# First layer of a four-layer attention program: where the instance norm's sums are taken, and by which engines

## The chip, the core and the metric

The program runs on 1 core of a Trainium2 chip. The metric is the device time of one execution in microseconds (us); lower is better. Before the change it is 4261.2 us, the median of 3 runs (4258.87 to 4265.15).

## What is computed

Four layers run one after the other on 8 batches; the change touches the first. With `x` and the context of 256 channels by 512 positions per batch, this layer projects queries, keys and values (16 heads of 16), takes a softmax attention over 512 positions, and uses its output's mean and spread to restyle the instance norm of `x`. The part that is changed is that norm:

```python
def _masked_instance_norm(x, mask):
    m = mask.astype(x.dtype)
    x = x * m
    n_valid = jnp.sum(m, axis=-1, keepdims=True)
    mean = jnp.sum(x, axis=-1, keepdims=True) / n_valid
    var = jnp.sum(x * x, axis=-1, keepdims=True) / n_valid - mean * mean
    x = (x - mean) / jnp.sqrt(jax.nn.relu(var) + EPS)
    return x * m
```

The output of the layer, per channel and position, is this norm times the root of the attention's variance (the attention of squared values less the squared attention, clipped at zero), plus the attention itself, times the mask.

## The kernel before

The layer is the function `layer0`. Five engines each run a hand-written list of instructions, tied together by semaphores. Heads are taken in 4 groups of 4 per batch, and every engine has a function `group(b, g)` with a loop over 8 steps `n`; in a step TensorE makes the scores of one pair of heads and one quarter of positions (`scores`, L481), the products whose maxima belong to the group after the next (`maxima`, L461), and weighted values of two steps before (`weighted`, L495). ScalarE takes the exponential of each step's scores (L653), VectorE the maxima (`take_max`, L764). TensorE may not start the next `maxima` before VectorE has read the last one, and not the scores of step n before the exponential of step n-2 is done. Everything else is hung into these steps at fixed places `n`: projections of the next batch in groups 0 and 2 (n = 3 and 4), values in group 3 (n = 5 and 7), transposes of a finished pair (`turn_pair`, L503) at n = 2 and 6. Groups 2, 3, 0, 1 of consecutive batches are the body of a hardware loop, so one period of the loop goes from group 2 of one batch to group 2 of the next.

The norm runs on the transposed rows `XT` (positions on partitions, 4 quarters of 128 positions by 256 channels), so that its result fits the attention's output:
- VectorE's `mask_x` (L801 to L807) copies the mask column and multiplies `XT` by it, half at the end of group 1, half in group 2, n = 0, and sets `stats_read`, after which SyncE may load the next `XT` (`load_statistics`).
- ScalarE squares the result into `XQ` in group 2, n = 5 (L673).
- TensorE's `statistics` (L439), at the end of group 2, multiplies both by a matrix of ones, so that every partition receives the sums over positions, for 256 channels each:

```python
for c in range(EC):
    pe.matmul(ps[:, BX, 0:L], ONES[:, :], XM[:, c, :], start=(c == 0), stop=(c == EC - 1), skip_group_check=True)
```

- VectorE's `moments` and `spread_of_x` (L809 to L822), in group 3, n = 0, scale the sums by the reciprocal of the valid count and form the variance, 256 columns wide. `count_valid` (L734) counts the mask on VectorE.
- GpSimd's `centre` (L323) subtracts the mean in group 3.
- ScalarE's `roots` (L681 to L685), in group 0 of the next batch behind n = 5 and the copy of that group's first pair, takes the root of the variance (256 columns) and of the attention's variance `VAR` (1024 columns). Each switch between exponential and root is a table load.
- VectorE's `inverse_root` (L874) takes reciprocals in two halves, GpSimd multiplies by `VAR` (L335), by the reciprocals (`scale`, L329), adds the attention (`shift`, L339), masks (L345) and stores.

For the last batch VectorE's `last_output` (L878) does all of the last part, and SyncE stores (L274). Layer 2 of the program starts behind that store.

SyncE issues nearly all transfers in one fixed order: in the loop, strips of group 1, maxima, `load_statistics`, `load_inputs`, queries and keys to scratch memory, strips of group 2, maxima, strips of group 3, and so on (L247 to L261). An entry that waits holds up all behind it.

## Time and profile before

| | |
|---|---|
| runs (3) | 4258.87, 4261.2, 4265.15 us |
| profiled execution | 4272.13 us, span 4270.5 us |
| mean granted clock of TensorE | 0.974 of full speed |
| TensorE busy in the span | 4003.9 us (94%) |
| VectorE, ScalarE, GpSimd busy | 2937.2, 1937.1, 1590.8 us |
| last store of the first layer issued at | 693.8 us |

The profile is of one execution. A row of a timeline gives start and duration in us, then engine, line, operation and tiles, and in brackets how long the engine sat idle before it and what ended that. Durations overlap a little: the next instruction of an engine often starts some 0.1 us before the last one's end. `PE` is TensorE, `DVE` VectorE, `ACT` ScalarE, `POOL` GpSimd, `SPq` SyncE's queue.

### The profile page before, as it was taken

The page shows a single profiled execution, that of the slowest core. Times are in us where ns is not written, and L with a number is a line of the kernel's source. Part 1 is how long each engine was busy: PE and PEld are TensorE (multiplying, and loading weights), DVE is VectorE, ACT ScalarE, POOL GpSimd, SP SyncE. Part 2 cuts the span into 40 slices and gives each one's busy share as a digit, 9 for nine tenths or more (in the row PEclk, how much of TensorE's full clock was granted, in tenths as well). Part 3 has the DMA queues.
Part 4 walks back from the last instruction along what each step waited for, and adds up shares of the span by engine and source line. Part 5 has one row for each costly group of instructions (what it writes and reads, how often), then busy time and mean ns, then how long its engine had stood idle before and what let it go on. Part 6 is the DMA issues. An engine that isn't in the chain of part 4 may idle for free. (4 is left out here: it accounts for less than half of the span.)

```text
span 4270.5 us, 68365 instructions
## 1 busy us (share of the span) xinstructions
PE 4003.9 (94%) x20812; PEld 3017.2 (71%) x20812; DVE 2937.2 (69%) x6467; ACT 1937.1 (45%) x3782; POOL 1590.8 (37%) x1094
## 2 busy tenths in 40 slices
PE   6999996789999987999999999999999999999999
PEld 2343333567777755887977888977988877878866
DVE  5667663688888893775757766757757757757643
ACT  2566563223333322555552555543555534555522
POOL 1334331456666651232235232344332244232230
PEclk7999998899999998999999999999999999999999
DMA  5434433000000002212123222223221122121122
GB/s 149 131 111 119 128 90 129 6 11 16 16 16 16 11 11 74 70 60 80 60 65 104 70 65 76 65 63 107 65 82 64 55 76 93 60 90 61 56 79 99
DMA packets 159994, 298.65 MB, mean 70 GB/s; under 512 B 19781, under 2 KB 42821, under 8 KB 158545
## 3 DMA queue, kind: packets, MB, share of 16 engines
q1 hardware_dynamic: 158000, 290.86, 21.9%
q0 software_dynamic: 1008, 3.67, 0.2%
q8 instruction: 119, 1.95, 0.2%
q10 hardware_dynamic: 752, 1.23, 0.1%
q14 instruction: 115, 0.93, 0.1%
HBM read 254.28 MB, written 42.21 MB: 69 GB/s over the span
## 5 line engine op out<-in xcount | busy, mean ns | idle before, releaser
L2177 POOL TENSOR_TENSOR c_wl<-c_wr,c_wh 128x512 fp32r<-128x512 f32 (+1 forms) x576 | 821.5, 1438 | 1641.9 <-ACT c_wh L2544 1385.2
L2645 ACT ACTIVATE c_pr<-c_ps,c_nms 128x257 f32<-128x257 f32 x512 | 244.5, 477 | 482.0 <-DVE c_nms L2867 480.1
L1701 DVE TENSOR_TENSOR_SCAN b_sb<-b_wt,b_s,b_ps 128x256 f32<-128x256 f32 x512 | 361.6, 736 | 16.3 <-PE b_ps L1154 4.4
L764 DVE TENSOR_REDUCE a_nm<-a_ps 128x2 f32<-128x1024 f32 x256 | 311.5, 1221 | 63.1 <-PE a_ps L461 61.2
L653 ACT ACTIVATE a_ex<-a_ps 128x1024 f32<-128x1024 f32 x256 | 260.3, 1023 | 181.4 <-PE a_ps L481 180.3
L1652 POOL TENSOR_TENSOR b_sb<-b_sb,b_rt 128x1024 f32<-128x1024 f32 x128 | 278.0, 2179 | 156.5 <-DVE b_sb L1701 122.4
L2544 ACT ACTIVATE c_wh<-c_wr 128x512 fp32r<-128x512 f32 (+1 forms) x464 | 315.3, 687 | 44.4 <-PE c_ps L2264 40.7
L2262 PE MATMUL c_ps<-c_hh,c_wh 128*128 128x512 f32 x768 | 309.6, 403 | 12.4 <-DVE c_hl L2751 12.0
L2262 PE MATMUL c_ps<-c_gh,c_wh 128*128 128x512 f32 x768 | 307.6, 400 | 5.4 <-DVE c_gl L2909 2.7
L2264 PE MATMUL c_ps<-c_hh,c_wl 128*128 128x512 f32 x768 | 304.5, 397 | 0.0
L2263 PE MATMUL c_ps<-c_hl,c_wh 128*128 128x512 f32 x768 | 304.2, 396 | 0.0
L2262 PE MATMUL c_ps<-c_wh,c_cth 128*128 128x256 f32 x1024 | 303.5, 296 | 0.0
L2264 PE MATMUL c_ps<-c_gh,c_wl 128*128 128x512 f32 x768 | 303.3, 395 | 0.0
L2263 PE MATMUL c_ps<-c_gl,c_wh 128*128 128x512 f32 x768 | 302.9, 394 | 0.0
L2264 PE MATMUL c_ps<-c_wh,c_ctl 128*128 128x256 f32 x1024 | 288.3, 282 | 0.0
L2263 PE MATMUL c_ps<-c_wl,c_cth 128*128 128x256 f32 x1024 | 287.7, 281 | 0.0
L495 PE MATMUL a_ps<-a_ex,a_vf 128*64 128x512 f32 x1024 | 278.6, 623 | 1.4 <-ACT a_ot L645 1.3
L2865 DVE TENSOR_REDUCE c_nm<-c_ps 128x1 f32<-128x257 f32 x512 | 215.1, 420 | 71.8 <-PE c_ps L2264 71.4
L1166 PE MATMUL b_ps<-b_xf,b_w 128*128 128x256 f32 x1056 | 244.1, 385 | 12.1 <-DVEq L1760 10.1
L1166 PEld LDWEIGHTS b_ps<-b_xf,b_w 128*128 128x128 f32 x1056 | 200.3, 192 | 46.3 <-issue 14.4
L2909 DVE TENSOR_TENSOR c_gl<-c_g,c_gh 128x512 fp32r<-128x512 f32 x128 | 90.7, 713 | 206.3 <-ACT c_gh L2627 206.1
L2861 DVE TENSOR_SCALAR c_pr<-c_pr,c_rs 128x257 f32<-128x257 f32 x512 | 195.0, 381 | 42.0 <-issue 3.1
(371 smaller groups left out, 10087.0 us busy)
## 6 DMA issues: line engine op xcount, KB each, us to landing
c_wr<-in_downs SPq DMA_DIRECT2D x192, 256.0 KB, 2.7
c_wr<-in_wv SPq DMA_DIRECT2D x64, 512.0 KB, 4.0
c_wr<-in_wk SPq DMA_DIRECT2D x128, 256.0 KB, 2.9
c_wr<-in_wq SPq DMA_DIRECT2D x128, 256.0 KB, 2.6
a_qp<-strips SPq DMA_DIRECT2D x64, 256.0 KB, 4.1
a_kp<-strips SPq DMA_DIRECT2D x64, 256.0 KB, 4.9
c_wr<-in_fc SPq DMA_DIRECT2D x64, 256.0 KB, 2.8
strips<-a_qh SPq DMA_DIRECT2D x32, 256.0 KB
```

The source lines that it names most:

```text
L495: mm = pe.matmul(ps[64 * a:64 * a + VCOLS, BO, :], VF[:, k, g * HG + 2 * p + a, :], EX[:, n % 4, a, :], start=(k == 0), stop=(k == EC - 1) ...
L653: act.activation(EX[:, n % 4, :, :], ps[:, BT + 2 * (n % 2):BT + 2 * (n % 2) + 2, :], ACT.Exp).then_inc(ex_ready, 1)
L764: dve.tensor_reduce(NM[:, s, :].rearrange("p (h c) -> p h c", h=HG)[:, 2 * p:2 * p + 2, c:c + 1], ps[:, bank:bank + 2, :], AX.X, ALU.max, ...
L1166: mm = pe.matmul(half(bank, o), W[:, w, k, o * P:(o + 1) * P], src[:, k, :], start=(k == 0), stop=(k == EC - 1), skip_group_check=True)
L1652: pool.tensor_tensor(SB[:, quad % RING, :, :, 0:L], SB[:, quad % RING, :, :, 0:L], RT[:, third(b, q // 8)].unsqueeze(1).broadcast_to([P, 2 ...
L1701: mm = dve.tensor_tensor_scan(SB[:, quad % RING, pr % 2, e, 1:L + 1], WT[:, third(b, i), e, :], half(spread_bank(pair), e), S0[:, b % 2, 2 ...
L2177: pool.tensor_tensor(piece(WL, slot), piece(WR, slot), piece(WH, slot), ALU.subtract).then_inc(piece_cut[slot], 1)
L2262: pe.matmul(out, sh, mh, start=start, stop=False, skip_group_check=True)
L2263: pe.matmul(out, sh, ml, start=False, stop=False, skip_group_check=True)
L2264: return pe.matmul(out, sl, mh, start=False, stop=stop, skip_group_check=True)
L2544: act.activation(piece(WH, slot), piece(WR, slot), ACT.Copy).then_inc(piece_high[slot], 1)
L2645: act.activation(PR[:, i, 0:L + 1], ps[:, BS + 1 - i % 2, 0:L + 1], ACT.Exp, bias=NMS[:, i:i + 1], scale=float(K2) ** -0.5, accum_out=RS[: ...
```

## The change

The sums are no longer taken from the transposed rows by TensorE, but from the rows `X` as they are loaded for the projections (channels on partitions, 2 halves of 128 by 512 positions), so that each sum is one column.
- VectorE's `sum_inputs` multiplies a half by the mask row and adds it up (one half at the end of group 1, one in group 2, n = 0, for the batch after). ScalarE's `square_inputs` squares the product with a sum (group 2, n = 1 and 2), `count_valid` moves to ScalarE (group 1, n = 4).
- ScalarE's `column_moments` (group 3, n = 3) scales the four sums and forms the clipped variance on columns; `roots` now takes the root of 2 columns of the same batch besides that of `VAR` of the batch before, VectorE's `inverse_root` the reciprocal of 2 columns (group 1, n = 6).
- TensorE's `statistics` transposes mean and reciprocal root, each column repeated 128 times, back into rows: four transposes. VectorE's `take_rows` copies them out.
- GpSimd's `normalize` subtracts and multiplies in group 3, from the unmasked `XT`; `centre` and `scale` go. `stats_read` is now set by its first product.
- SyncE's `load_statistics` stands behind group 0's maxima instead of ahead of `load_inputs`; `load_inputs` waits for `x_summed` and `counted`.
- The conversions `cut_x` and `cut_c` on ScalarE are made in halves, `square_values` moves from n = 2 to n = 6, in group 0 ahead of `cut_c`; GpSimd's `cut_c` stands ahead of `copy_values(b, 1)`.
- For the last batch GpSimd does the first three groups' part of the output, VectorE the last group's, after waiting for GpSimd.

The diff, cut to its core:

```diff
@@ load_inputs, SyncE
-                sp.wait_ge(mask_read, b + AHEAD)
+                sp.wait_ge(x_summed, b * LC + AHEAD)
+                sp.sem_inc(passed, 1)
+                sp.wait_ge(counted, b + AHEAD)
@@ SyncE's loop
                 place_maxima(b, 3)
-                load_statistics(b + 1)
                 load_inputs(b + 2)
...
                 place_maxima(b + 1, 0)
+                load_statistics(b + 1)
                 place_strips(b + 1, 3)
@@ GpSimd
+            def normalize(b):
+                pool.wait_ge(st_read, b + 1 + AHEAD)
+                pool.wait_ge(stats_x_in, (b + 1) * N_STATS + AHEAD)
+                pool.tensor_tensor(XM[:, :, :], XT[:, :, :], ST[:, 0:1, :].broadcast_to([P, EC, L]), ALU.subtract)
+                pool.drain().then_inc(stats_read, 1)
+                pool.tensor_tensor(XM[:, :, :], XM[:, :, :], ST[:, 1:2, :].broadcast_to([P, EC, L]), ALU.mult)
...
+            cols = slice(0, (G0 - 1) * CG)
+            pool.wait_ge(std_ready, B + AHEAD)
+            pool.tensor_tensor(XM[:, :, cols], XM[:, :, cols], VAR[:, :, cols], ALU.mult)
+            pool.tensor_tensor(XM[:, :, cols], XM[:, :, cols], MEAN[:, :, cols], ALU.add)
+            for c in range(EC):
+                pool.tensor_scalar(OUT[:, c, cols], XM[:, c, cols], MCOL[:, c:c + 1], None, ALU.mult)
+            pool.drain().then_inc(parts_out, 1)
@@ statistics, TensorE
-                for c in range(EC):
-                    pe.matmul(ps[:, BX, 0:L], ONES[:, :], XM[:, c, :], start=(c == 0), stop=(c == EC - 1), skip_group_check=True)
-                for c in range(EC):
-                    mm = pe.matmul(ps[:, BX, L:2 * L], ONES[:, :], XQ[:, c, :], start=(c == 0), stop=(c == EC - 1), skip_group_check=True)
+                for i, k in itertools.product(range(2), range(LC)):
+                    mm = pe.transpose(ps[:, BX, i * L + k * P:i * L + (k + 1) * P], COLS[:, i, k:k + 1].broadcast_to([P, P]), ID[:, :])
@@ ScalarE
+            def count_valid(b):
+                act.activation(JUNK[:, :], M8R[:, :], ACT.Copy, accum_out=NV[:, :]).then_inc(counted, 1)
+            def column_moments(b):
+                act.wait_ge(rn_ready, b + 1 + AHEAD)
+                act.wait_ge(x_squared, (b + 1) * LC + AHEAD)
+                act.wait_ge(st_ps, b + AHEAD)
+                act.activation(COLS[:, :, :], SUMS[:, :, :], ACT.Copy, scale=RN[:, 0:1])
+                act.drain()
+                act.activation(MSQ_X[:, :], COLS[:, 0, :], ACT.Square)
+                act.drain()
+                for k in range(LC):
+                    act.activation(COLS[:, 1, k:k + 1], MSQ_X[:, k:k + 1], ACT.Relu, scale=-1.0, bias=COLS[:, 1, k:k + 1])
+                act.drain()
+            def square_inputs(b, k):
+                act.wait_ge(x_summed, b * LC + k + 1 + AHEAD)
+                act.activation(XS[:, k, :], XS[:, k, :], ACT.Square, accum_out=SUMS[:, 1, k:k + 1]).then_inc(x_squared, 1)
-                act.activation(ST[:, 3, :], ST[:, 2, :], ACT.Sqrt, bias=EPS[:, 0:1])
+                act.activation(COLS[:, 1, :], COLS[:, 1, :], ACT.Sqrt, bias=EPS[:, 0:1]).then_inc(root_x, 1)
@@ VectorE
+            def sum_inputs(b, k):
+                if k == 0:
+                    dve.wait_ge(inputs_in, (b + 1) * N_IN + AHEAD)
+                dve.tensor_tensor_reduce(XS[:, k, :], X[:, k, :], M8R[:, :], 1.0, 0.0, ALU.mult, ALU.add, SUMS[:, 0, k:k + 1]).then_inc(x_summed, 1)
+            def inverse_root(b):
+                dve.reciprocal(COLS[:, 1, :], COLS[:, 1, :]).then_inc(cols_ready, 1)
+            def take_rows(b):
+                dve.wait_ge(st_ps, b + 1 + AHEAD)
+                dve.tensor_copy(ST[:, :, :], ps[:, BX, :].rearrange("p (s t) -> p s t", s=2)).then_inc(st_read, 1)
```

How the order moves, on TensorE at the end of group 2: `L481` are scores, `L461` products for maxima, `L495` weighted values, `L446` and `L448` the products with ones. Before:

```order
L503 MATMUL a_ps<-a_id,a_ot 128x128 x4
L477 REGISTER_ALU
L481 MATMUL a_ps<-a_qp,a_kp 128x512 x2
L458 REGISTER_ALU
L461 MATMUL a_ps<-a_kp,a_qp 128x512 x2
L495 MATMUL a_ps<-a_ex,a_vf 64x512 x2
L441 REGISTER_ALU
L446 MATMUL a_ps<-a_xm,a_ones 128x256 x4
L448 MATMUL a_ps<-a_xq,a_ones 128x256 x4
L475 ISA
L477 ISA
L481 MATMUL a_ps<-a_qp,a_kp 128x512 x2
```

And now (`L460` are the transposes of the columns):

```order
L515 MATMUL a_ps<-a_id,a_ot 128x128 x4
L489 REGISTER_ALU
L493 MATMUL a_ps<-a_qp,a_kp 128x512 x2
L470 REGISTER_ALU
L473 MATMUL a_ps<-a_kp,a_qp 128x512 x2
L507 MATMUL a_ps<-a_ex,a_vf 64x512 x2
L456 REGISTER_ALU
L460 MATMUL a_ps<-a_id,a_cols 128x128 x4
L487 ISA
L489 ISA
L493 MATMUL a_ps<-a_qp,a_kp 128x512 x2
```

Eight products of 256 columns gave way to four of 128; nothing else moved on TensorE. On VectorE, at the border of groups 1 and 2 (the loop begins at the branch; `a_nm` are the maxima), before:

```order
L764 TENSOR_REDUCE a_nm<-a_ps 128x2
L801 CAST a_mcol<-a_m8c 128x4
L804 TENSOR_SCALAR a_xm<-a_xT,a_mcol 128x256 x2
L925 UNCONDITIONAL_BRANCH
L925 ISA
L764 TENSOR_REDUCE a_nm<-a_ps 128x2
L804 TENSOR_SCALAR a_xm<-a_xT,a_mcol 128x256 x2
L763 REGISTER_ALU
L764 TENSOR_REDUCE a_nm<-a_ps 128x2
```

And now:

```order
L829 TENSOR_REDUCE a_nm<-a_ps 128x2
L783 ISA a_xs,a_sums<-a_x,a_m8r 128x512
L783 ISA a_sums 128x1
L945 UNCONDITIONAL_BRANCH
L945 ISA
L829 TENSOR_REDUCE a_nm<-a_ps 128x2
L783 ISA a_xs,a_sums<-a_x,a_m8r 128x512
L783 ISA a_sums 128x1
L828 REGISTER_ALU
L829 TENSOR_REDUCE a_nm<-a_ps 128x2
```

Each pair of masked quarters became one multiply-and-sum in two instructions, and the mask column's copy left this place.

## Rows read from the trace of the kernel before

**Rows 1.** Windows, one period: PE, PEld, DVE, ACT, POOL busy, clock, DMA share, GB/s

```profile
340.08:418.81 78.73, 75.20 (x357) 30.83 (x357) 54.66 (x75) 47.29 (x56) 30.23 (x31) 1.00 0.41 122
```

**Rows 2.** TensorE's groups by line, 200 to 650 us: busy, mean ns, idle before

```profile
L461 PE MATMUL a_ps<-a_kp,a_qp 64*128 64x512 f32 x368 | 81.8, 441 | 12.6 <-DVE a_nm L764 12.6
```

**Rows 3.** Timeline of TensorE, 340 to 402 us: the rows with a wait

```profile
340.08 0.51 PE L461 MATMUL a_ps<-a_kp,a_qp 64*128 64x512 f32 x2 [0.65 <-DVE a_nm L764]
...
363.33 0.49 PE L461 MATMUL a_ps<-a_kp,a_qp 64*128 64x512 f32 x2 [0.32 <-DVE a_nm L764]
...
365.74 0.49 PE L461 MATMUL a_ps<-a_kp,a_qp 64*128 64x512 f32 x2 [0.27 <-DVE a_nm L764]
...
400.38 0.50 PE L481 MATMUL a_ps<-a_qp,a_kp 64*128 64x512 f32 x2 [1.09 <-ACT a_ex L653]
```

**Rows 4.** Timeline of TensorE, end of group 2

```profile
354.92 0.66 PE L503 MATMUL a_ps<-a_id,a_ot 128*128 128x128 f32 x4
355.51 0.50 PE L481 MATMUL a_ps<-a_qp,a_kp 64*128 64x512 f32 x2
...
357.18 1.99 PE L446 MATMUL a_ps<-a_xm,a_ones 128*128 128x256 f32 x8
...
360.83 0.51 PE L481 MATMUL a_ps<-a_qp,a_kp 64*128 64x512 f32 x2
```

**Rows 5.** Timeline of VectorE, groups 1 to 3

```profile
336.21 1.23 DVE L764 TENSOR_REDUCE a_nm<-a_ps 128x2 f32<-128x1024 f32 x1
...
338.82 1.21 DVE L764 TENSOR_REDUCE a_nm<-a_ps 128x2 f32<-128x1024 f32 x1
...
363.19 0.42 DVE L817 TENSOR_TENSOR a_st<-a_st 128x256 f32<-128x256 f32 x1
```

**Rows 6.** Groups by line and form, VectorE and ScalarE, whole span

```profile
L793 DVE TENSOR_TENSOR a_vs<-a_ps,a_bvb 128x512 f32<-128x512 f32 x16 | 11.1, 692 | 25.1 <-PE a_ps L436 25.1
...
L1817 DVE SCALAR_TENSOR_TENSOR b_zb<-b_zb,b_xb 128x1024 f32<-128x1024 f32 x6 | 7.3, 1218 | 0.0
...
L2645 ACT ACTIVATION_READ_ACCUMULATOR c_pr<-c_ps,c_nms 128x1 f32 x512 | 98.7, 193 | 0.0
```

**Rows 7.** Timeline of ScalarE, then one row of TensorE, groups 3 and 0

```profile
369.97 1.02 ACT L653 ACTIVATE a_ex<-a_ps 128x1024 f32<-128x1024 f32 x1 [0.56 <-PE a_ps L481]
...
383.92 0.60 ACT L645 ACTIVATE a_ot<-a_ps 128x512 f32<-128x512 f32 x1
...
395.24 1.28 ACT L683 ACT_TABLE_LOAD   x1
396.54 0.51 ACT L683 ACTIVATE a_st<-a_st,a_eps 128x256 f32<-128x256 f32 x1
...
399.30 1.02 ACT L653 ACTIVATE a_ex<-a_ps 128x1024 f32<-128x1024 f32 x1
...
374.69 0.50 PE L481 MATMUL a_ps<-a_qp,a_kp 64*128 64x512 f32 x2
```

**Rows 8.** Tail of the layer: ScalarE, SyncE; GpSimd's masking by line

```profile
685.54 0.83 ACT L715 ACTIVATE a_var<-a_var 128x768 f32<-128x768 f32 x1
...
693.82 0.35 SPq L274 DMA_DIRECT2D x1T<-a_xq  x1
...
L345 POOL TENSOR_SCALAR a_xq<-a_xm,a_mcol 128x256 f32<-128x256 f32 x28 | 25.4, 918 | 1.2 <-issue 1.2
```

**Rows 9.** GpSimd and SyncE in group 3; first batch's head; the page's issues

```profile
371.58 2.38 POOL L323 TENSOR_TENSOR a_xm<-a_xm,a_st 128x1024 f32<-128x1024 f32 x1
...
377.54 1.31 SPq L224 DMA_DIRECT2D a_qp<-strips  x2
...
12.46 2.35 POOL L294 TENSOR_TENSOR a_cl<-a_ctx,a_ch 128x1024 fp32r<-128x1024 f32 x1 [9.56 <-ACT a_ch L631]
...
12.78 2.18 DVE L729 TENSOR_SCALAR a_mbrr<-a_m8r 128x256 fp32r<-128x256 uint8 x1 [0.20 <-issue]
...
a_kp<-strips SPq DMA_DIRECT2D x64, 256.0 KB, 4.9
```

More of the change, by code:

```diff
@@ L97, in layer0 @@
         ID = sb("id", [P, P])
-        ONES = sb("ones", [P, P])
         EPS = sb("eps", [P, 1])
@@ L116, in layer0 @@
         MSQ = sb("msq", [P, EC, HG, D0])
-        ST = sb("st", [P, 4, L])
+        ST = sb("st", [P, 2, L])
         NV = sb("nv", [P, 1])
         RN = sb("rn", [P, 1])
+        SUMS = sb("sums", [P, 2, LC])
+        COLS = sb("cols", [P, 2, LC])
+        MSQ_X = sb("msq_x", [P, LC])
+        XS = sb("xs", [P, 2, E])
+        JUNK = sb("junk", [P, E])
         OUT = XQ
@@ L653, in group @@
                     act.activation(EX[:, n % 4, :, :], ps[:, BT + 2 * (n % 2):BT + 2 * (n % 2) + 2, :], ACT.Exp).then_inc(ex_ready, 1)
+                    if g == 0 and n == 0 and not first:
+                        square_values(b, 0)
+                    if g == 0 and more and n == 0:
+                        cut_c(b + 1, 0)
+                        cut_c(b + 1, 1)
                     if n == 1 and not first:
@@ L658, in group @@
                             take_pair(b - 1, G0 - 1, 1)
[L659 to L661 removed]
+                    if n == 6 and g + 1 < G0:
                         square_values(b, g + 1)
+                    if g == 2 and more and n in (1, 2):
+                        square_inputs(b + 1, n - 1)
+                    if g == 1 and more and n == 4:
+                        count_valid(b + 1)
                     if more and g % 2 == 0 and n == QUERIES_AT:
@@ L668, in group @@
                         keys(b + 1, g // 2)
-                    if g == 2 and n == 5:
-                        act.wait_ge(stats_in, b + 1 + AHEAD)
-                        act.wait_ge(out_free, b + AHEAD)
-                        act.activation(XQ[:, :, :], XM[:, :, :], ACT.Square).then_inc(sq_ready, 1)
-                    if g == 0 and n == 0 and not first:
-                        square_values(b, 0)
-                    if g == 0 and n == 5 and prior is not None:
-                        roots(prior)
@@ L678, in group @@
-                    if g == G0 - 1 and n == 5 and further:
-                        cut_x(b + 2)
-            def roots(b):
-                act.wait_ge(var_x, b + 1 + AHEAD)
-                act.activation(ST[:, 3, :], ST[:, 2, :], ACT.Sqrt, bias=EPS[:, 0:1])
-                act.wait_ge(var_v, (b + 1) * G0 + AHEAD)
-                act.activation(VAR[:, :, :], VAR[:, :, :], ACT.Sqrt).then_inc(std_ready, 1)
+                    if g == G0 - 1 and more and n == 3:
+                        column_moments(b + 1)
@@ new lines, in group @@
+                    if g == 0 and n == 5:
+                        roots(b, prior)
+                    if g == G0 - 1 and n in (5, 6) and further:
+                        cut_x(b + 2, n - 5)
+            def count_valid(b):
+                act.wait_ge(inputs_in, (b + 1) * N_IN + AHEAD)
+                act.activation(JUNK[:, :], M8R[:, :], ACT.Copy, accum_out=NV[:, :]).then_inc(counted, 1)
[10 more added lines that the diff above has]
+                act.drain()
@@ L687, in _ @@
             act.wait_ge(wqk_in, 16 + AHEAD)
             act.activation(WH[:, :, :, 1, :], WQK[:, :, :, 1, :], ACT.Copy).then_inc(wk_high, 1)
-            cut_x(0)
-            cut_c(0)
+            for k in range(LC):
+                cut_x(0, k)
+            for k in range(LC):
+                cut_c(0, k)
             act.wait_ge(weights_split, 2 + AHEAD)
@@ L695, in _ @@
             keys(0, 1, BT + 3)
+            count_valid(0)
             square_values(0, 0)
-            cut_x(1)
+            for k in range(LC):
+                square_inputs(0, k)
+            column_moments(0)
+            for k in range(LC):
+                cut_x(1, k)
             group(0, 0, first=True)
@@ L826, in group @@
                     if g == G0 - 1 and n == 0:
-                        moments(b)
+                        take_rows(b)
                     if left > 1:
@@ L850, in group @@
                         mask_rows(1, 1)
-                    if first and n == 5:
-                        count_valid(1)
                     if g == G0 - 1 and further and n == 1:
@@ L915, in _ @@
             dve.tensor_tensor(WVL[:, :, :], WV, WVH[:, :, :], ALU.subtract).then_inc(wv_split, 1)
+            for k in range(LC):
+                sum_inputs(0, k)
+            count_inverse(0)
             take_values(0, 0, BO)
```

158 lines of the change are left out of this document (62 added, 96 removed).

## The prediction

> **What bounds the kernel.** The change touches only the first layer, the first 694 of 4270.5 us, so I read the windows of that layer first. One batch repeats every 78.73 us, and TensorE is busy for 75.20 of them, at a granted clock of 1.00, that is 2.4 GHz; VectorE has 54.66, ScalarE 47.29, GpSimd 30.23 [rows 1]. TensorE is the bound, and its order is written out by hand, so what is taken from it or from its waits shortens the loop one for one, as long as nobody else becomes late. Second, TensorE's groups by line between 200 and 650 us (5.7 batches) tell what it waits for ahead of the products whose maxima VectorE takes: 12.6 us for VectorE, nothing for a transfer [rows 2]. Third, its timeline shows where in a batch these waits lie. Four bear on the change: 0.65 us at 340.08, 0.32 at 363.33, 0.27 at 365.74, and, for ScalarE's exponential, 1.09 at 400.38 [rows 3]. The first is also the start of the next period (it comes back at 418.81).
>
> **The change, part by part.** All times are of the batch between 340 and 419 us; the other six like it are the same to some hundredths.
>
> *Column sums on TensorE.* The eight products with the matrix of ones start at 357.18 (the first four in 8 passes), and the next scores start at 360.83: 3.65 us. In their place stand four transposes of 128 columns. The four of a pair of heads, same shape and type, start at 354.92 and let the next product start at 355.51: 0.59 us [rows 4]. That the stationary side is one column repeated has no row; bounds are 0.59 and, if each went in two passes as the ones' products do, 1.2. I take 0.59, the same form. 3.06 us less, in all 8 batches (the last too: nothing else runs on TensorE there), is 24.5 us; with 1.2 it is 19.6.
>
> *VectorE at the border of groups 1 and 2.* The last maximum of group 1 ends at 337.44 (336.21 + 1.23), then mask column and two masked quarters run, the first maximum of group 2 starts only at 338.82, and TensorE waits 0.65 us for its end [rows 5, 3]. Now one multiply-and-sum of 128x512 stands there, and another after that maximum. No row shows the form. Lower bound: one pass, a two-input operation of 128x512, 0.69; upper: two passes, 1.38. The order shows a second instruction that fetches the sum; VectorE has no row of one, ScalarE's takes 0.19 [rows 6]. I take one pass, 0.69 + 0.16 less 0.1 of overlap, 0.75: two-input operations are the nearest rows, and all of them run in one pass. Then the first maximum starts at 338.2, ends at 339.4, and TensorE, which comes at 339.43, hardly waits: 0.6 won. The second sum ends at 340.2 and the maximum behind it at 341.4, about when TensorE asks again (a step later; two such steps lie 2.4 us apart between 363.33 and 365.74, and this one is a little shorter): free. In 7 batches (the last takes no maxima there): 4.2 us. Upper bound of the price: 1.4 each gives back all of the 0.6 and adds 0.6 at the next maximum, so 4.2 less and 4.2 more lost, 8.4 between the ends.
>
> *VectorE at the start of group 3.* Two scaled copies, two products, a clip, and a reciprocal become one copy of 128x512, about 0.68 by its width [rows 6]. Both waits come from them: the first maximum came behind the scaled copies, the second behind the variance from 363.19 [rows 5]. With 0.7 the first wait shrinks to about 0.1, the second goes: 0.49 in 7 batches, 3.4 us. If the copy takes 1.0, 0.3 a batch comes back (2 us).
>
> *ScalarE at the roots.* Table load 1.28, root of the moments' 256 columns (0.51 busy, 0.41 to the next start), root of the values, load, and the exponential at 399.30 holds TensorE 1.09 us [rows 7, 3]. The first root now has 2 columns, about 0.2 (ScalarE's smallest form takes 0.19 [rows 6]), 0.1 of it overlapped: 0.3 less, 7 times, 2.1 us. The added roots in the very first group cost 2.8 us of ScalarE; the later ones (4.1 us) overrun TensorE by 1.09, so 3.0 is free, and this costs nothing. If that cover were gone, 2.8 once.
>
> *ScalarE elsewhere.* The halved conversion of the context costs one extra start, 0.12, right ahead of the pair copy of 383.92 [rows 7], for which TensorE is just in time: 0.1 x 7, 0.7 us lost. Count of the mask, two squares with sum (0.63 + 0.19 each) and the column work (four of 0.2, and three drains, no row, 0 to 0.3 each: 0.8 to 1.7) fall into steps with one exponential of 1.02 us, in an engine that is idle for 31 of 78.7 us; the exponential behind the column work starts at 369.97 and ends 1.02 later, and the scores that need it come at 374.69 [rows 7], so up to 3.7 us are hidden. The square of the masked rows (1.05) goes. Nothing on the path.
>
> *GpSimd and queues.* Centring and scaling stay two products of 2.38; both are now in group 3, so the output is stored some 5 us earlier. The load of rows and mask column moved behind a maximum's placement, and waits for GpSimd's first product: a rival below. The inputs' load comes one transfer sooner. All hidden under TensorE.
>
> *Head and tail.* Head: conversions in halves, 0.1; the sums lie in VectorE's 3 us of idle time before the first values. Tail: before, the store is issued at 693.82. Now ScalarE's root of 768 columns ends 0.41 earlier, at 685.96; GpSimd then does two products of 768 columns (3/4 of 2.38, 1.78 each) and four of 192 (0.69 to 0.92 each), so 6.3 to 7.2 us, to 692.3 to 693.2; VectorE, waiting for it, adds two operations of 256 columns (0.42 each) and four small ones: store at 693.9 to 695.6 [rows 8, 5]. I take 1.2 us lost: this part gains nothing, GpSimd is the slower engine for it.
>
> Sum: 24.5 + 4.2 + 3.4 + 2.1 - 0.7 - 1.2 = **32.3 us less**. The profiled execution took 4272.1 us, 10.9 above the median shown; against the median, 4261.2 - 32.3 = **4228.9**.
>
> **A rule weighed.** In the first batch VectorE took 2.18 us for 256 columns of mask rows, where a two-input operation of 512 takes 0.69 [rows 6], and it ended (14.96) as GpSimd's product of 12.46 did (14.81) [rows 9]: the two engines do block each other. The new sums read two SBUF tensors. In before GpSimd worked until 339.6 at this place, because its output chain waited for VectorE's reciprocals; without scaling there it is done 3.5 us before the sums, so I charge nothing. If it overlapped, its step of 0.74 us would be added, at most 7 x 0.7 = 5 us. The Trainium skill, page "SBUF — State Buffer", in its practical consequences, says that a VectorE instruction with two SBUF inputs contends with a GpSimd instruction that reads SBUF, the later one waiting in full; by it alone the overlapping case holds and the sum is 27. The trace agrees with blocking (2.18 us); where GpSimd will be is the open point.
>
> **Rivals.**
> *A, the sums are slow on VectorE.* Two passes, 1.4 us each: VectorE delays TensorE in two steps. 32.3 - 8.4 = 23.9, time **4237**. For it: the form has no row and carries an accumulator. Against: the product of two 128x512 tensors and the maxima over 1024 columns run in one pass. The Trainium skill, "Vector Engine (DVE) Microarchitecture Reference", in its list of pitfalls, says that this family with two SBUF sources that are not bf16 runs at half throughput, leaving no port for the accumulator; by that rule this rival is the outcome. A three-operand form of 128x1024 takes 1218 ns here [rows 6], which is full rate, but without an accumulator.
>
> *B, transposes cost double.* 24.5 becomes 19.6: **4234**.
>
> *C, slower: the SyncE queue stands behind GpSimd.* The load of rows and mask column now waits on SyncE for GpSimd's first product, which in before ran from 371.58 to 373.96. Behind it is queued the placement of group 3's strips, issued at 377.54 in before [rows 9]. TensorE asks for these strips at about 400.7; issuing the four takes 2.6 (twice 1.31) and landing 4.9 [rows 9], so the placement may slip to about 393, and the product's end, with 1.2 us for two issues, to about 392: 18 us later than now. Beyond that point each us costs 7. To eat 32.3 us it would have to be 23 us late. GpSimd has 48 us idle in a batch and depends there only on pair 1 of group 2 and on the copied rows, so I see no way; if it does happen, with 28 us of delay, the time is about **4299** (7 x 10 - 32.3 more).
>
> *D, no change:* freed TensorE time returns as waits on transfers. TensorE waited for none in the loop; 4261.
>
> **How the numbers follow.** The sum as it stands, 4224 to 4234: 0.58. A, including port blocking: 0.27. B: 0.06. More than summed (further waits for VectorE go too, tail even): 4221, 0.03. C: 0.02, slower. D: 0.04. The predicted time is 4229. The range, 4221 to 4241, takes in A and B with 2 to 4 us for their own bounds. A measurement of this kernel tells 0.2% (8.5 us) from no change: faster 0.94, same 0.04, slower 0.02.
>
> **What would show it.** Right: the transposes of the columns start 0.6 us ahead of the next scores; period 74.3 to 74.5 us; no wait left at the two places of group 3 and at the border of groups 1 and 2; the wait after the roots near 0.8; the store of the last batch 30 to 33 us earlier than 693.82. Wrong: a multiply-and-sum above 1.2 us and a wait in its place (A); transposes over 1 us together (B); TensorE waiting for strips in group 1 (C), or for any transfer (D).

## The result, and the profile after

The changed kernel took **4228.4 us**, median of 4 runs (4223.6 to 4230.6), beside 4262.1 us for the kernel before in the same comparison (4258.9 to 4265.2): a ratio of 0.9916, with a 95% interval of 0.9904 to 0.9928. That is 31 to 41 us less, 33.7 by the medians. Measured twice more, it gave 4228.3 (ratio 0.9916, 0.990 to 0.9933) and 4231.4 us (0.9927, 0.9914 to 0.9941).

The period of the loop is now 73.80 us instead of 78.73 [rows 1]. The windows view of one (here from the wait behind the keys in group 2 to the same place of the next batch), with the columns of [rows 1]:

```profile
337.27:411.07 73.80, 71.62 (x345) 28.25 (x346) 51.29 (x68) 48.80 (x67) 30.15 (x31) 1.00 0.44 129
```

TensorE is busy for 3.58 us less (75.20 to 71.62), VectorE for 3.37, ScalarE for 1.51 more. The other 1.35 us of the 4.93 are time in which TensorE waited. In its groups by line, 200 to 620 us (about the same 5.7 batches as [rows 2], now shorter), idle time for VectorE fell from 12.6 to 6.0 us:

```profile
L493 PE MATMUL a_ps<-a_qp,a_kp 64*128 64x512 f32 x370 | 92.2, 495 | 6.0 <-ACT a_ex L671 6.0
L473 PE MATMUL a_ps<-a_kp,a_qp 64*128 64x512 f32 x362 | 79.0, 433 | 6.3 <-DVE a_nm L829 6.0
```

TensorE's timeline at the end of group 2 and the start of group 3. The four transposes start at 340.96 and the next scores 0.58 us behind them, where 3.65 passed before [rows 4], and the two waits of 0.32 and 0.27 in group 3 [rows 3] are gone. The wait of 0.60 in the first row is none of these: it stands behind the low halves of the keys, and the kernel before had it too, at 353.49, with the same length.

```profile
337.27 0.49 PE L473 MATMUL a_ps<-a_kp,a_qp 64*128 64x512 f32 x2 [0.60 <-DVE a_nm L829]
...
340.96 0.65 PE L460 MATMUL a_ps<-a_id,a_cols 128*128 128x128 f32 x4
341.54 0.50 PE L493 MATMUL a_ps<-a_qp,a_kp 64*128 64x512 f32 x2
...
343.21 0.50 PE L493 MATMUL a_ps<-a_qp,a_kp 64*128 64x512 f32 x2
343.60 0.50 PE L473 MATMUL a_ps<-a_kp,a_qp 64*128 64x512 f32 x2
...
345.25 0.50 PE L493 MATMUL a_ps<-a_qp,a_kp 64*128 64x512 f32 x2
345.58 0.39 PE L473 MATMUL a_ps<-a_kp,a_qp 64*128 64x512 f32 x2
```

Later in the period two more waits are left, one behind the keys in group 0 and one behind the roots, the latter 0.88 us instead of 1.09. The three are all that the period has in brackets:

```profile
375.33 0.50 PE L473 MATMUL a_ps<-a_kp,a_qp 64*128 64x512 f32 x2 [0.60 <-DVE a_nm L829]
...
379.98 0.50 PE L493 MATMUL a_ps<-a_qp,a_kp 64*128 64x512 f32 x2 [0.88 <-ACT a_ex L671]
```

The 0.65 at the border of groups 1 and 2 is gone, though not to the last tenth. The product for the maxima starts 0.57 us behind its scores there, where an undisturbed step of this kind has 0.38 (349.17 and 349.56, for one), so some 0.2 us of waiting is left that no bracket shows:

```profile
323.40 0.49 PE L493 MATMUL a_ps<-a_qp,a_kp 64*128 64x512 f32 x2
323.97 0.50 PE L473 MATMUL a_ps<-a_kp,a_qp 64*128 64x512 f32 x2
```

VectorE where the first of the two new sums stands (one batch), and the copy that starts group 3:

```profile
322.08 0.69 DVE L783 CUSTOM_DVE_ANT_0 a_xs<-a_x,a_m8r 128x512 f32<-128x512 f32 x1 [0.18 <-issue]
322.69 0.08 DVE L783 DVE_READ_ACCUMULATOR2_ANT a_sums<- 128x1 f32 x1
322.69 1.22 DVE L829 TENSOR_REDUCE a_nm<-a_ps 128x2 f32<-128x1024 f32 x1
...
341.65 0.69 DVE L795 COPY a_st<-a_ps 128x512 f32<-128x512 f32 x1 [0.34 <-PE a_ps L460]
```

The multiply-and-sum is one pass: 0.69 us, and 0.08 for the read of its sum; the copy is 0.69. Over the whole trace the sixteen sums lie between 678 and 692 ns.

ScalarE at the roots. The root of two columns takes 0.29 us, where the 256 columns that it replaced took 0.51 [rows 7]: only 0.22 us went with the other 254.

```profile
375.05 1.28 ACT L724 ACT_TABLE_LOAD   x1
376.34 0.29 ACT L724 ACTIVATE a_cols<-a_cols,a_eps 128x2 f32<-128x2 f32 x1
376.55 1.04 ACT L727 ACTIVATE a_var<-a_var 128x1024 f32<-128x1024 f32 x1
377.61 1.28 ACT L671 ACT_TABLE_LOAD   x1
378.90 1.02 ACT L671 ACTIVATE a_ex<-a_ps 128x1024 f32<-128x1024 f32 x1
```

**Where the 33.7 us lie.** The profiled executions of before and after differ by more than the medians, so two marks are used that are in every trace: the first statistic product (or transpose) of batch 0, and the issue of the layer's last store.

| us | before | after | difference |
|---|---|---|---|
| first statistic pass | 121.0 | 119.5 | -1.5 |
| last store issued | 693.82 | 655.63 | -38.2 |
| between the two | 572.8 | 536.1 | **-36.7** |
| from the store to the end of the span | 3576.7 | 3566.3 | -10.4 |
| span | 4270.5 | 4221.9 | -48.6 |

The two profiled executions differ by 48.6 us, since that of before came out long. The stretch between the marks is the one that repeats: in two more executions of the changed kernel it was 536.1 and 536.2 us. Of before only this one execution was profiled, and it holds 1.4 us that belong to no term. Behind the last roots TensorE waits 1.81 us, until 633.75, and its next instructions are slow; the granted clock between 636.0 and 637.4 is 0.50 of full speed, that is 1.2 GHz:

```profile
634.41 1.93 PE L495 MATMUL a_ps<-a_ex,a_vf 128*64 128x512 f32 x4
```

Elsewhere this row takes 1.08 us. The kernel of experiment 1 has the same wait of 1.81 there and no slow stretch behind it, and no profiled execution of the changed kernel has one in this layer. The start of the layer varied over 2.6 us between the three executions of the changed kernel, and what comes behind the store, where no instruction changed, lay between 3566 and 3577 us over all the kernels below. So the layer gained 36.7 us between the marks, 35.3 without the slow stretch, and the medians 33.7; the interval of the latter (31 to 41) holds both. The experiments are read by the stretch between the marks, with the medians beside it.

### The profile page after: what moved, and what is told of

It is laid out like the page before. It is cut to its first block and busy times, and to the rows that moved or that the text cites. A ratio compares the mean times of both kernels' runs of the same rounds, so it can differ in the third digit from the quotient of the medians.

```text
span 4221.9 us, 68235 instructions
## 1 busy us (share of the span) xinstructions
PE 3965.2 (94%) x20716; PEld 2988.3 (71%) x20716; DVE 2910.6 (69%) x6417; ACT 1949.7 (46%) x3872; POOL 1601.2 (38%) x1100
```

## The experiments

My theory at this point: the gain is the sum of the terms, with TensorE's 3.07 us a batch by far the largest, and VectorE and GpSimd hidden. Rivals: the gain needs the sums' place on VectorE and not the shorter passes; or the layer is now bound by waits so that more or less TensorE work no longer tells.

**1. Only fewer products.** The kernel before, with two of the eight products with ones; it leaves out three quarters of each column sum and keeps all else.

```diff
-                for c in range(EC):
-                    pe.matmul(ps[:, BX, 0:L], ONES[:, :], XM[:, c, :], start=(c == 0), ...)
-                for c in range(EC):
-                    mm = pe.matmul(ps[:, BX, L:2 * L], ONES[:, :], XQ[:, c, :], start=(c == 0), ...)
+                pe.matmul(ps[:, BX, 0:L], ONES[:, :], XM[:, 0, :], start=True, stop=True, ...)
+                mm = pe.matmul(ps[:, BX, L:2 * L], ONES[:, :], XQ[:, 0, :], start=True, stop=True, ...)
```

> The kernel before, with only one of the four quarters in each of the two column sums: two products with ones instead of eight (the sums of three quarters of the positions are left out, nothing else moves). Theory, TensorE's time counts one for one and the other gains are VectorE's and ScalarE's own: the two products take 0.9 us instead of 3.65, the period falls by 2.7 from 78.73 to 76.0, the two long steps at the start of group 3 (2.47 and 2.79 us) and the one at the border of groups 1 and 2 stay, the time falls by 22 us, to about 4240. Rival, the freed time returns in waits on VectorE, whose scaled copies and variance still follow: the steps of group 3 grow, and less than 11 us are won.

Measured: 4246.4 us, ratio 0.9957 (0.9941 to 0.9974). Between the marks 550.9 us, 21.9 less than before. Its TensorE timeline, from the last products of the statistics:

```profile
348.81 0.59 PE L446 MATMUL a_ps<-a_xq,a_ones 128*128 128x256 f32 x2
349.33 0.50 PE L479 MATMUL a_ps<-a_qp,a_kp 64*128 64x512 f32 x2
...
351.83 0.51 PE L459 MATMUL a_ps<-a_kp,a_qp 64*128 64x512 f32 x2 [0.32 <-DVE a_nm L762]
...
354.24 0.51 PE L459 MATMUL a_ps<-a_kp,a_qp 64*128 64x512 f32 x2 [0.26 <-DVE a_nm L762]
...
388.89 0.51 PE L479 MATMUL a_ps<-a_qp,a_kp 64*128 64x512 f32 x2 [1.08 <-ACT a_ex L651]
```

The two products that are left take 1.06 us until the next scores (348.27 to 349.33) instead of 3.65, so 2.59 us are spared, 20.7 in 8 batches. The other 1.2 us are the slow stretch that only the profiled execution of before has (1.4), less small changes of other steps. What TensorE is spared arrives in the time one for one, with the waits of [rows 3] in place at nearly their old lengths (0.63 for the 0.65). So six of the eight products carry 20.7 us, and the waits are a gain of their own.

**2. More transposes.** The changed kernel, with the four transposes issued six times over.

```diff
-                for i, k in itertools.product(range(2), range(LC)):
+                for _, i, k in itertools.product(range(6), range(2), range(LC)):
```

> The changed kernel with the four transposes made six times over: 20 more at 0.147 us, so 2.94 us of TensorE given back per batch, nothing else. Theory: the period rises from 73.81 to 76.75, the time by 23.5 us, to about 4252; the steps at the start of group 3 stay at 2.04 and 2.25 us, so that the rest of the gain (about 10 us against the kernel before) remains. Rival, the gain hangs on VectorE's shorter lists alone: the time stays near 4228.

Measured: 4249.1 us, ratio 0.9964 (0.995 to 0.9978). Between the marks 553.7 us, 17.6 more than the changed kernel, where I had expected 23.5:

```profile
345.45 2.83 PE L460 MATMUL a_ps<-a_id,a_cols 128*128 128x128 f32 x24
348.21 0.50 PE L493 MATMUL a_ps<-a_qp,a_kp 64*128 64x512 f32 x2
```

24 of them take 2.76 us until the next scores, the first four 0.58: each further one costs (2.76 - 0.58) / 20 = 0.11 us. My expectation had 0.147, the 0.59 divided by four, which spreads the group's fixed part over its members. The added 2.18 us are 17.4 in 8 batches, and 17.6 came. TensorE is still the bound in the changed kernel, one for one, and rival B has no ground.

**3. Sums twice.** The changed kernel, each multiply-and-sum preceded by one into a tile of no use.

```diff
+                dve.tensor_tensor_reduce(XD[:, k, :], X[:, k, :], M8R[:, :], 1.0, 0.0, ALU.mult, ALU.add, SD[:, k:k + 1])
                 dve.tensor_tensor_reduce(XS[:, k, :], X[:, k, :], M8R[:, :], 1.0, 0.0, ALU.mult, ALU.add, SUMS[:, 0, k:k + 1]).then_inc(x_summed, 1)
```

> The changed kernel with every multiply-and-sum on VectorE made twice (the first one into tiles that nobody reads): 0.69 us more at each of the two places. Theory, VectorE stands right behind TensorE at the border of groups 1 and 2, and a sum of 1.4 us is what my rival A priced: TensorE waits about 0.6 us at each of the two steps, the period rises by 1.2, the time by 8.4, to about 4237. Rival, VectorE has 24 us idle per period and takes it in: no change, 4228.

Measured: 4240.4 us, ratio 0.9943 (0.9926 to 0.9959). Between the marks 542.7 us, 6.6 more. Two waits appeared at the border:

```profile
402.89 0.50 PE L475 MATMUL a_ps<-a_kp,a_qp 64*128 64x512 f32 x2 [0.68 <-DVE a_nm L832]
...
405.25 0.50 PE L475 MATMUL a_ps<-a_kp,a_qp 64*128 64x512 f32 x2 [0.21 <-DVE a_nm L832]
```

They make 0.89 us. By distance the two steps are 1.09 us longer (0.61 and 0.48), and six of the seven borders lie between the marks, the first batch's ahead of them: 6.4 of the 6.6 us. This is the price that rival A would have had, not 8.4: VectorE works 0.62 us longer at each of the two places, 1.24 together, and behind the second sum there was 0.1 to 0.2 us of slack.

**4. The tail on VectorE.** GpSimd's share of the last batch's output moved to VectorE, the masking in one operation of 256 columns for each part instead of 192 and 64. The last rows of the changed kernel's layer, GpSimd's and VectorE's:

```profile
646.71 1.86 POOL L404 TENSOR_TENSOR a_xm<-a_xm,a_var 128x768 f32<-128x768 f32 x1 [4.14 <-ACT a_var L762]
646.99 1.73 DVE L913 TENSOR_SCALAR a_var<-a_msq 128x256 f32<-128x256 f32 x1
648.71 1.80 POOL L406 TENSOR_TENSOR a_xm<-a_xm,a_mean 128x768 f32<-128x768 f32 x1
648.75 0.42 ACT L764 ACTIVATE a_var<-a_var 128x256 f32<-128x256 f32 x1 [2.22 <-DVE a_var L913]
650.69 2.99 POOL L409 TENSOR_SCALAR a_xq<-a_xm,a_mcol 128x192 f32<-128x192 f32 x4 [0.18 <-issue]
653.76 0.43 DVE L916 TENSOR_TENSOR a_xm<-a_xm,a_var 128x256 f32<-128x256 f32 x1 [5.04 <-POOLq L410]
...
655.63 0.35 SPq L283 DMA_DIRECT2D x1T<-a_xq  x1
```

VectorE waits 5.04 us for an engine that does the same work at half its rate.

```diff
-            pool.tensor_tensor(XM[:, :, cols], XM[:, :, cols], VAR[:, :, cols], ALU.mult)
...
-            pool.tensor_tensor(XM[:, :, cols], XM[:, :, cols], MEAN[:, :, cols], ALU.add)
...
-                pool.tensor_scalar(OUT[:, c, cols], XM[:, c, cols], MCOL[:, c:c + 1], None, ALU.mult)
...
+                dve.tensor_tensor(XM[:, :, first], XM[:, :, first], VAR[:, :, first], ALU.mult)
...
+                dve.tensor_tensor(XM[:, :, first], XM[:, :, first], MEAN[:, :, first], ALU.add)
...
-                    dve.tensor_scalar(OUT[:, c, cols], XM[:, c, cols], MCOL[:, c:c + 1], None, ALU.mult)
+                    dve.tensor_scalar(OUT[:, c, :], XM[:, c, :], MCOL[:, c:c + 1], None, ALU.mult)
```

> The changed kernel with the whole output of the last batch on VectorE again (no reciprocals there, since the scaling is done in group 3), nothing on GpSimd. Theory, the tail lost because GpSimd takes 6.6 us for what VectorE does in 3.4 and they work one after the other: the store is issued at 651.5 to 652.5 instead of 655.6, the time falls by 3.5 us. Rival, the tail waits for ScalarE's roots anyway: no change in the store.

Measured: 4226.4 us, ratio 0.9912 (0.9895 to 0.9928), beside 4228.3 and 0.9916 for the changed kernel on the same chip. The medians can't tell them apart; between the marks it is 531.75 us, 4.35 less, where 3 to 4 were expected. The end of VectorE's timeline:

```profile
644.65 0.29 DVE L904 TENSOR_SCALAR a_var<-a_msq 128x256 f32<-128x256 f32 x1
644.86 0.95 DVE L908 TENSOR_TENSOR a_xm<-a_xm,a_var 128x768 f32<-128x768 f32 x1
...
647.60 1.14 DVE L916 TENSOR_SCALAR a_xq<-a_xm,a_mcol 128x256 f32<-128x256 f32 x4
```

768 columns take 0.95 us here and 1.86 on GpSimd. The first row shown took 1.73 us in the changed kernel (646.99 to 648.72), while GpSimd's product stood beside it (646.71 to 648.57), and 0.29 here with GpSimd idle.

**5. The keys one step later.** The two waits of 0.60 us left for VectorE stand right behind the low halves of the keys; here VectorE makes these a step later.

```diff
-                    if more and g % 2 == 0 and n == KEYS_AT:
+                    if more and g % 2 == 0 and n == KEYS_AT + 1:
```

> The changed kernel with VectorE's low part of the keys taken behind the maximum of step 5 instead of ahead of it. Theory, the waits of 0.60 us of TensorE in groups 0 and 2 (337.27, 375.33) come from a maximum that stands behind the keys, which wait for ScalarE: both go, the period falls by 1.2 to 72.6, the time by 8 to 9 us. Rival, the keys' later low part delays the transposes of step 6, which wait for it: no gain.

Measured: 4221.3 us, ratio 0.9899 (0.9883 to 0.9916). Between the marks 531.9 us, 4.2 less than the changed kernel, half of what was expected. Both waits went, and the one for ScalarE took over half of it:

```profile
372.85 0.50 PE L493 MATMUL a_ps<-a_qp,a_kp 64*128 64x512 f32 x2 [1.55 <-ACT a_ex L671]
```

0.88 became 1.55. By distance, each step whose wait of 0.60 went is 0.68 us shorter. In group 2 this is won, 4.1 us in the six batches whose keys lie between the marks. In group 0 all 0.68 come back one step later, at the roots. ScalarE's chain of copy, load, root, root, load and exponential does not depend on the keys' low halves; TensorE simply arrives at it earlier.

**6. The roots ahead of the keys.** The same wait from the other side: ScalarE takes the roots one step earlier, and the pair's copy behind the keys' high halves.

```diff
-                    if n == 5:
+                    if n == 5 and g > 0:
                         take_pair(b, g, 0)
+                    if g == 0 and n == KEYS_AT:
+                        roots(b, prior)
                     if more and g % 2 == 0 and n == KEYS_AT:
                         keys(b + 1, g // 2)
+                    if g == 0 and n == KEYS_AT:
+                        take_pair(b, g, 0)
...
-                    if g == 0 and n == 5:
-                        roots(b, prior)
```

> The changed kernel with ScalarE's roots moved from behind step 5's pair copy to ahead of the keys' conversion in step 4, where TensorE projects and ScalarE is idle for 1.7 us; the first pair's copy comes right behind the keys. Theory: the wait of 0.88 us in group 1 goes, and at most 0.3 us comes back before the transposes of step 6: the period falls by 0.6 to 0.9, the time by 4 to 6 us. Rival, the keys come 2 us late and TensorE waits for them: no gain or slower.

Measured: 4230.1 us, ratio 0.9914 (0.9898 to 0.9931), no difference from the changed kernel. Between the marks 535.5 us, 0.6 less, where 4 to 6 were expected. ScalarE's wait is gone, and VectorE's in the same group grew from 0.60:

```profile
375.45 0.50 PE L473 MATMUL a_ps<-a_kp,a_qp 64*128 64x512 f32 x2 [1.36 <-DVE a_nm L831]
```

VectorE's low halves need ScalarE's high halves, which now come behind the roots; its maxima stand behind them. By distance, 0.94 us a batch are won at the roots, 0.76 lost at the maxima and 0.17 in the step behind. Experiments 5 and 6 together say that group 0's wait behind the keys and the wait behind the roots are one knot: whichever is taken alone, the other grows. The wait behind the keys of group 2 is no part of it.

**7. The rows queued early.** Rival C in one move: on SyncE, the load of rows and mask column goes ahead of the placement of group 2's strips and of group 0's maxima. It can't go as far ahead as in the kernel before, where it stands ahead of the inputs. By the code, its release needs GpSimd's product, and this comes behind moments that VectorE takes only behind the next mask rows (`mask_rows`), which wait for the inputs and for keys written by entries behind it on this queue. That was read from the code, not run.

```diff
+                load_statistics(b + 1)
                 place_strips(b + 1, 2)
                 place_maxima(b + 1, 0)
-                load_statistics(b + 1)
                 place_strips(b + 1, 3)
```

> The changed kernel with the load of the transposed rows two entries earlier on SyncE, ahead of the strips of group 2 and the maxima that follow, still waiting for GpSimd's first product. This is the mechanism of my rival C with its slack taken away. Theory: strips and maxima go out only after the product's end (353.7 in the changed kernel) and land at about 362, where TensorE asks at 360: some 2.3 us of waits on a transfer in each of 7 batches, the time up by 16 us, to about 4244. Rival, nothing is behind it in time: 4228.

Measured: 4265.8 us, ratio 1.0002 (0.9992 to 1.0012). Between the marks 573.6 us, 37.5 more than the changed kernel: this one move gives the whole gain back, where I had expected 16. SyncE's timeline in it, then two rows of TensorE's:

```profile
375.03 0.36 SPq L186 DMA_DIRECT2D a_m8c<-in_mask_col  x1
375.61 0.39 SPq L187 DMA_DIRECT2D a_xT<-in_xT  x1
376.29 1.30 SPq L233 DMA_DIRECT2D a_qp<-strips  x2
377.64 1.24 SPq L233 DMA_DIRECT2D a_kp<-strips  x2
379.08 2.62 SPq L196 DMA_DIRECT2D a_qp<-a_nmT  x4
```

```profile
384.92 0.50 PE L493 MATMUL a_ps<-a_qp,a_kp 64*128 64x512 f32 x2 [3.80 <-DMA a_qp<-a_nmT]
...
385.58 1.97 PE L507 MATMUL a_ps<-a_ex,a_vf 128*64 128x512 f32 x4
```

The load leaves when GpSimd's first product is done (372.37 + 2.38 = 374.75), and strips and maxima follow in one block, the strips 18.0 us behind the wait at the keys of group 2 (358.30); TensorE reaches the scores that need these maxima 3.80 us too soon.

That wait is not the whole cost. The second row is an instruction that takes 1.08 us in the changed kernel. While TensorE stood (380.9 to 384.9) its granted clock was 1.00; between 387.0 and 388.6 it was 0.50, the lower of its two levels, 1.2 GHz, and from 390 on 1.00 again. The edit stands in the loop, which runs 6 times. All six times TensorE waits, for 3.80 to 5.34 us, and the steps behind the wait are 1.3 to 2.7 us longer than in the changed kernel. The waits lengthen their steps by 27.0 us in all, the slow steps add 10.9. My expectation had the waits too short (2.3 us each), one batch too many, and no slow stretch at all.

In the changed kernel the same strips left at 344.20, 6.9 us behind that wait, and the maxima at 346.99, both before that product (351.32 to 353.69). The load followed it by 0.29 us without holding up anybody:

```profile
353.98 0.36 SPq L186 DMA_DIRECT2D a_m8c<-in_mask_col  x1
354.55 0.38 SPq L187 DMA_DIRECT2D a_xT<-in_xT  x1
357.28 1.30 SPq L233 DMA_DIRECT2D a_qp<-strips  x2
```

The queue is free again at 354.93, and the next strips wait for a reason of their own until 357.28: 2.35 us of slack, before a transfer that TensorE needs much later.

**8. All three.** Experiments 4, 5 and 6 in one kernel.

> The changed kernel with the three edits of the last call together: tail on VectorE, keys' low part behind the maximum of step 5, roots ahead of the keys' conversion. Apart, the later keys took away both waits of 0.60 us but raised the wait for ScalarE from 0.88 to 1.55, and the earlier roots took that wait away but raised the one for VectorE from 0.60 to 1.36. Theory, each hides what the other left: no wait of TensorE above 0.3 us in the period, which falls by 2.1 us, the tail by 4.4 us, so the time by 19 us, to about 4209. Rival, the late keys now hold up the transposes of step 6: less than 9 us.

Measured: **4214.6 us** (4212.2 to 4217.9), ratio 0.9884 (0.9869 to 0.990), beside 4231.4 and 0.9927 (0.9914 to 0.9941) for the changed kernel on the same chip. Between the marks 522.8 us: 13.4 less than the changed kernel and 50 less than before. The parts alone sum to 4.35 + 4.2 + 0.6 = 9.2. The knot in group 0 is worth 4.9 us when both of its waits are taken, and 0 and 0.6 when one is; group 2's wait gives 4.1 here as in experiment 5, the tail 4.5. The one wait of the period that is left:

```profile
372.51 0.50 PE L484 MATMUL a_ps<-a_qp,a_kp 64*128 64x512 f32 x2 [0.67 <-ACT a_ex L662]
```

I had expected 19 us, with all waits gone. 0.67 in six batches is 4.0 of the missing 5.6, and one pair of the waits behind the keys that I had counted seven times, 1.2, lies outside the marks.

**9. GpSimd beside the sums.** The changed kernel, with three products of 128x1024 on GpSimd behind its copy of the values in group 2, which nobody reads.

```diff
+                for _ in range(3):
+                    pool.tensor_tensor(PD[:, :, :], PS[:, :, :], PS[:, :, :], ALU.mult)
+                    pool.drain()
```

> The changed kernel with three idle products of 128x1024 on GpSimd (7.2 us, into a tile that nobody reads) behind the copy of group 3's values, so that GpSimd reads SBUF while VectorE makes its two sums (322.1 to 324.5 in the changed kernel); GpSimd is otherwise idle from 318.7 to 328.9. Theory, the two-input sums wait for the GpSimd product that has started: a sum is recorded with up to 2.4 us more, TensorE waits in group 2, and the time rises by 7 to 20 us, to 4235 to 4248. Rival, they do not meet: 4228 and sums of 0.69 us.

Measured: 4237.2 us, ratio 0.9942 (0.9927 to 0.9957). Between the marks 542.3 us, 6.2 more, a little under the 7 to 20 expected. VectorE, then GpSimd:

```profile
324.78 1.15 DVE L789 CUSTOM_DVE_ANT_0 a_xs<-a_x,a_m8r 128x512 f32<-128x512 f32 x1 [0.17 <-issue]
...
327.00 1.23 DVE L789 CUSTOM_DVE_ANT_0 a_xs<-a_x,a_m8r 128x512 f32<-128x512 f32 x1
```

```profile
323.49 4.19 POOL L379 TENSOR_TENSOR a_pd<-a_pdum 128x1024 f32<-128x1024 f32 x2 [0.24 <-issue]
```

Two GpSimd products lie in that row. The second ends at 327.68, and the second sum, begun at 327.00, ends at 328.23, 0.55 later. The first product, taken by itself, is 1.89 us long; it ended at 325.38, and the first sum at 325.93, again 0.55 later. A sum alone takes 0.69, so it did nearly all of its work after its neighbour was done. The maxima between, 1.21 us, read no SBUF and are not lengthened beside the same products. The ten sums between 200 and 600 us averaged 1259 ns instead of 685. The two steps of TensorE at the border grew by 0.4 to 0.8 and by 0.3 to 0.4 us at each of the six borders between the marks, together 6.1 us, and no other step did: the 6.2 us are the price of the blocked sums.

## Why the prediction was right

The forecast was 4229 us, and 4228.4 came; its sum was 32.3 us, the layer gave 36.7, or 35.3 without the slow stretch of before, and the medians 33.7. Part of the closeness is luck: the terms fell short by 3 us, and the medians by less. Two of the prediction's own signs missed on the good side, the period (73.80 us, not 74.3 to 74.5) and the last store (38.2 us earlier, not 30 to 33). Point by point, in its own steps; the measured column adds up the steps of TensorE between the marks, from one score to the next, batch by batch:

| term, us | forecast | measured | by |
|---|---|---|---|
| column sums on TensorE | 24.5 | 24.6 | 3.65 to 0.58, 8 times |
| border of groups 1 and 2 | 4.2 | 4.2 | 0.57 + 0.18 in most of the 6 between the marks |
| start of group 3 | 3.4 | 6.5 | 0.97, 7 times, less in the last |
| roots | 2.1 | 1.5 | 1.09 to 0.88, 7 times |
| context in halves | -0.7 | -0.4 | -0.07, 6 times |
| all other steps | none | 0.2 | each below 0.1 a batch |
| slow stretch of before | none | 1.4 | once, in this execution |
| tail | -1.2 | -1.25 | last moments to store, 8.49 to 9.74 |
| sum | 32.3 | 36.7 | 36.7 between the marks |

*Column sums: right in size and mechanism.* The transposes of a repeated column start 0.58 us ahead of the next scores, as those of a pair do (0.59 [rows 4]). Experiment 1 shows that such time comes out of the loop one for one, experiment 2 that it still does in the changed kernel.

*Border: right, with two errors that cancel.* The wait is nearly gone, as forecast. The step with the wait shrank by 0.57 us, and the one behind it, which I had put as free, by 0.18. I counted seven batches; the first one's border lies ahead of the first mark and had only a wait of 0.26. The multiply-and-sum, taken as 0.75, is 0.69 + 0.08.

*Start of group 3: the term that was mis-sized most.* I took TensorE's recorded waits, 0.32 + 0.27, less 0.1 for a rest of the first. No rest stayed, and the two steps shrank by 0.97 (2.47 to 2.04 and 2.79 to 2.25), more than the waits recorded in them. The rows say why. Without a wait the product for the maxima starts 0.33 us behind its scores, before these end (345.25 and 345.58), and is itself recorded at 0.39; with the wait of 0.27 it took 0.49 [rows 3]. The bracket counts only from where the engine stood empty; the overlap that is lost ahead of the wait, and the slower first product behind it, are in none of the brackets. This, and the like at the border, is also why TensorE's busy time fell by 3.58 and not by the 3.07 of the transposes. The measure for a step is the distance from its scores to the next.

*What I left unnamed.* Of VectorE's 12.6 us in [rows 2] I placed 0.65 + 0.32 + 0.27 a batch and said nothing of the rest: two waits of 0.60 behind the keys, which the change does not touch. They are the 6.0 us left in the view of after, and experiment 5 removed both, though it won only one.

*Roots.* 0.3 was forecast with a root of 0.2 us; it took 0.29, and 0.21 was won.

*Context in halves: right.* A cost of 0.1 a batch was forecast. The step at the pair copy of group 0, behind the halved conversion, is 2.33 us long instead of 2.26, in each of the six batches that convert a context there.

*Tail: right, with its cause.* 1.2 us lost because GpSimd is the slower engine; experiment 4 wins 4.35 by giving the work back to VectorE.

*The rule weighed.* The blocking counts only where GpSimd works beside the sums. In the changed kernel it doesn't, so nothing was lost, as charged. Experiment 9 puts it there, and 6.2 us go, more than the 5 I had as a most, since both sums of a batch are held up. The Trainium skill, page "SBUF — State Buffer", in its practical consequences, says that an instruction of VectorE with two SBUF inputs and one of GpSimd that reads SBUF hold each other off; experiment 9 agrees (1.26 us instead of 0.69). The 1.73 us instead of 0.29 in the tail, and the mask rows of the first batch [rows 9] on which I rested, are of instructions with a single SBUF input; they were held up as well, and that sentence says nothing of them.

*Rival A fell on the duration.* 0.69 us with f32 and uint8 sources from SBUF and an accumulator. The Trainium skill, page "Vector Engine (DVE) Microarchitecture Reference", in its points that are easy to get wrong, has an instruction form with two sources, `S2S2D2_STT`, at half throughput for such sources; the 0.69 us don't agree, if the multiply-and-sum is of that form, which its row (`CUSTOM_DVE_ANT_0`) does not tell. Experiment 3 prices the rival at 6.6 us.

*Rival B fell:* 0.58 for the four.

*Rival C is a real mechanism, and I had its nearest case wrong.* I looked at one entry behind the load, the placement of group 3, and gave it some 18 us of slack by TensorE's demand. No run tests these 18 us. Experiment 7 shows 6.2 us a batch lost when two more entries stand behind the load. Its load follows the same product as in the changed kernel; only the number of transfers that wait behind it differs. So the bad case was nearer than "no way": not a delay of 23 us but a move by two entries. The price was wrong too: "each us costs 7" left out the slow stretch behind each long wait.

*Rival D fell:* no wait on a transfer is in the changed kernel's period.

What stays open: the 1.6 us between the layer's gain of 35.3 and that of the medians, which the spread of the rest of the program (some 10 us between executions) hides; what decides whether a slow stretch follows a wait of 1.81 us; and ScalarE's last 0.67 us in experiment 8.

## What to carry to other kernels

Where one engine is the bound and its order is fixed, price an edit by the distance between its recurring instructions before and after, not by busy sums or by the waits in the rows: these gave 0.59 us where 0.97 was won. Account for the whole idle column of the group view; a remainder without an owner (6 us here) is the next thing to win, and two waits within one step of each other should be taken together, since each alone moved into the other (0 and 0.6 us alone, 4.9 together). On a queue that issues in order, what an added wait costs is set by what stands behind it: the same load cost nothing behind group 0's maxima and 37.5 us two entries further ahead. A long wait of TensorE can cost more than its length: 27 us of waits brought 11 us of slow steps with them. And count the batches between the marks for each term; seven, six and eight all occur here.

## What the runs showed of the hardware

- A multiply-and-sum on VectorE with two SBUF sources of 512 columns (f32, uint8) takes 686 ns (678 to 692), and the read of its accumulator 81 ns, where ScalarE's read takes 193 [rows 6].
- Beside GpSimd's products (experiment 9) the same instruction took 1.14 to 1.46 us in 13 of 16 cases, and ended 0.55 us after the neighbour's end in the cases read; VectorE's maxima over PSUM were not lengthened (1.21 us). A one-input operation of 256 columns was held up as well, 1.73 us instead of 0.29.
- GpSimd's product of 128x1024 took 1.89 us where both operands were one tile (experiment 9; up to 2.16 beside the sums) and 2.37 with two.
- A transpose of 128 columns in a row of others costs TensorE 0.11 us at a granted clock of 1.00 (experiment 2), and a root of 2 columns costs ScalarE 0.29 us.
- After TensorE had waited 3.80 to 5.34 us, its granted clock fell to 0.50 soon after it worked again, and the next steps took 1.3 to 2.7 us longer (experiment 7, six times of six). After waits of 1.81 us this happened once (before) and once not (experiment 1); after waits of 1.6 us and less in this layer it was not seen.
